# Four key products in other PSUM banks, in a two-layer graph kernel

## What is computed

```python
def layer0(h, adj):                       # Wq, Wk, Wv with biases
    query, key, value = h @ Wq.T + bq, h @ Wk.T + bk, h @ Wv.T + bv
    weight = adj * exp(query @ key.T)
    weight = weight / sum(weight, axis=2, keepdims=True)
    return weight @ value

def layer1(h, adj):
    agg = adj @ h / maximum(sum(adj, -1), 1e-6)
    return relu(concatenate([h, agg], axis=2) @ W.T)

x = x + layer0(maximum(layernorm(x), 0), adj)
x = x + layer1(maximum(layernorm(x), 0), adj)
```

## Time and profile before

| | us |
|---|---|
| median of 3 runs (2077.85 to 2078.81) | 2078.81 |
| span of the profiled execution | 2075.8 |
| TensorE busy in it | 2033.4 (98%) |
| DVE busy | 1420.9 (68%) |
| GpSimd busy | 1015.8 (49%) |
| ScalarE busy | 772.6 (37%) |

### The profile page before, as it was taken

How to read it: one execution, slowest core, us unless ns; L and a number is a source line. 1 busy time by engine, 2 the same in 40 slices (tenths; PEclk the granted TensorE clock), 3 DMA queues, 4 the chain that set the end, 5 groups by cost and what they waited for, 6 DMA issues and landing times.

```text
span 2075.8 us, 28517 instructions
## 1 busy us (share of the span) xinstructions
PE 2033.4 (98%) x9852; PEld 1702.4 (82%) x9852; DVE 1420.9 (68%) x2329; ACT 772.6 (37%) x1289; POOL 1015.8 (49%) x958
## 2 busy tenths in 40 slices
PE   8899999999999999999999999999999999999999
PEld 5688888888888888888888888888888888888887
DVE  6877676776667776767767677766677676767654
ACT  3433434333343334343333433344433334333432
POOL 3555553554544555535555445455355554454520
PEclk9999999999999999999999999999999999999999
DMA  5121122212222221222122221212221222212101
GB/s 188 61 76 67 66 76 91 81 51 76 72 85 81 70 72 66 76 91 81 51 72 75 86 81 65 76 66 76 91 81 51 71 76 86 81 60 82 63 29 51
DMA packets 114753, 155.30 MB, mean 75 GB/s; under 512 B 10800, under 2 KB 75312, under 8 KB 114736
## 3 DMA queue, kind: packets, MB, share of 16 engines
q1 hardware_dynamic: 114736, 155.08, 22.0%
HBM read 121.38 MB, written 33.68 MB: 75 GB/s over the span
## 4 chain that ended last, share of the span: by engine, by line
PE 87%; DVE 10%; issue 1%; DMA 0%; SPq 0%; ACT 0%; DVEq 0%; ACTq 0%
PE bank L337 28%; PE bank L339 28%; PE bank L338 28%; DVE hT_l L689 4%; PE bank L345 3%; DVE y L800 1%; DVE x L815 1%; DVE sums L834 1%; DVE h L831 1%; DVE h L730 0%; DMA x_in<-x 0%; DVE sum_inv L836 0%; DVE w_l L175 0%; DVE w L745 0%; DVE v_l L684 0%
## 5 line engine op out<-in xcount | busy, mean ns | idle before, releaser
L292 POOL TENSOR_TENSOR xT<-xT,shared 128x512 f32<-128x512 f32 x248 | 455.5, 1874 | 162.0 <-DMA shared<-norms 162.0
L325 POOL TENSOR_TENSOR at_l<-adjT,at_h 128x1024 fp32r<-128x1024 f32 x32 | 81.4, 2545 | 308.4 <-ACT at_h L675 308.4
L337 PE MATMUL bank<-hT_h,n_h 128*128 128x512 f32 x512 | 204.0, 399 | 23.6 <-DVE x L815 23.1
L269 POOL TENSOR_TENSOR rs<-var_eps,minus_half 128x2 f32<-128x2 f32 x128 | 89.7, 701 | 272.4 <-DVE var_eps L706 272.4
L730 DVE CUSTOM_DVE_ANT_0 h<-h,u_b,bqk 128x512 f32<-128x512 f32 x128 | 215.0, 1731 | 0.0
L535 ACT ACTIVATE h<-x,rs 128x512 f32<-128x512 f32 x124 | 94.1, 807 | 313.5 <-POOL rs L275 313.5
L579 ACT ACTIVATE y<-bank 128x512 f32<-128x512 f32 x128 | 76.7, 599 | 355.6 <-PE bank L339 355.6
L175 POOL TENSOR_TENSOR w_l<-w,w_h 128x512 fp32r<-128x512 f32 x62 | 80.4, 1297 | 255.1 <-ACT w_h L597 255.1
L338 PE MATMUL bank<-hT_l,n_h 128*128 128x512 f32 x512 | 200.3, 391 | 0.0
L339 PE MATMUL bank<-hT_h,n_l 128*128 128x512 f32 x512 | 200.1, 391 | 0.0
L337 PE MATMUL bank<-wv_h,hT_h 128*128 128x512 f32 x512 | 199.2, 389 | 0.0
(11 more groups left out here) (125 smaller groups left out, 4865.9 us busy)
## 6 DMA issues: line engine op xcount, KB each, us to landing
x_in<-x SPq DMA_DIRECT2D x32, 1024.0 KB, 5.3
xT<-x_t SPq DMA_DIRECT2D x62, 512.0 KB, 6.6
out<-x SPq DMA_DIRECT2D x124, 256.0 KB, 2.0
adjT<-adj_t SPq DMA_DIRECT2D x32, 512.0 KB, 3.5
shared<-adj SPq DMA_DIRECT2D x32, 512.0 KB, 4.8
shared<-norms SPq DMA_DIRECT2D x31, 512.0 KB, 3.6
x<-wq SPq DMA_DIRECT2D x4, 256.0 KB, 3.8
xb<-wk SPq DMA_DIRECT2D x4, 256.0 KB, 4.4
```

The costliest lines, as they stand in the source:

```text
L269: pool.tensor_tensor(rs[n][:, 0, tiles], var_eps[n][:, tiles], minus_half[:, :], ALU.pow).then_inc(rstd_done[n], 1)
L292: pool.tensor_tensor(tile, tile, norms[:, k * T:(k + 1) * T, :], (ALU.mult, ALU.add)[k]).then_inc((xT_scaled, xT_shifted)[k], 1)
L325: pool.tensor_tensor(at_l[:, :, :], adjT[:, :, :], at_h[:, :, :].bitcast(F32), ALU.subtract).then_inc(at_split, 1)
L337: pe.matmul(dst, lh, rh, start=first, stop=False)
```

## The change

The four key products get a list of banks of their own, 7, 4, 5 and 2. Their readers, line 569 on ScalarE and line 776 on DVE, read there. The waits of TensorE follow the last reader of each bank: in the steps with layer 1, kp(0) waits only for hT_split, kp(1) for ha_copied, kp(2) for y_done, and kp(3) for the first x1_done. turn_g(1), which writes bank 7, waits for the first kz_l. scores(0) and scores(1) write banks 0 and 1, and the first of them now waits for all four x1_done. In step 0, kp(1) waits for the copies of the bias columns and kp(2) for u_done. The order of instructions is the same on every engine; on TensorE a few register instructions that serve the waits come and go.

```diff
@@ -35,6 +35,7 @@
 L0_BANK, L1_BANK, TR_BANK = 0, 4, 6
+KP_BANK = (7, 4, 5, 2)
@@ -382,11 +383,22 @@
                 def kp(dt):
-                    pe.wait_ge(hT_split, DT * (i + 1))
-                    if layer1:
-                        pe.wait_ge(x1_done, T * j + dt + 1)
+                    if dt == 0:
+                        pe.wait_ge(hT_split, DT * (i + 1))
+                    elif dt == 1:
+                        if not layer1:
+                            pe.wait_ge(bias_columns_done, 2)
+                        elif not first:
+                            pe.wait_ge(ha_copied, T * j)
+                    elif dt == 2:
+                        if not layer1:
+                            pe.wait_ge(u_done, 1)
+                        elif not first:
+                            pe.wait_ge(y_done, T * j)
+                    elif layer1:
+                        pe.wait_ge(x1_done, T * j + 1)
                     cols = slice(dt * P, (dt + 1) * P)
-                    product(bank[L0_BANK + (dt + 2) % 4][:, :],
+                    product(bank[KP_BANK[dt]][:, :],
                             [(n_h[:, c, cols], n_l[:, c, cols], hT_h[:, c, :], hT_l[:, c, :]) for c in range(DT)]
                             ).then_inc(kp_psum, 1)
@@ -407,6 +419,8 @@
                         if g == 0 and kt == 0:
+                            if layer1:
+                                pe.wait_ge(x1_done, T * (j + 1))
                             pe.wait_ge(kp_split, DT * i + DT - 1)
                             product(dst, terms[:-1], stop=False)
                             pe.wait_ge(kp_split, DT * (i + 1))
@@ -485,6 +499,7 @@
                     kp(3)
                     if layer1:
                         turn_g(j, 0)
+                        pe.wait_ge(kp_split, DT * i + 1)
                         turn_g(j, 1)
                     scores(0)
@@ -566,7 +581,7 @@
-                    nc.scalar.activation(kz_h[:, dt, :], bank[L0_BANK + (dt + 2) % 4][:, :], ACT.Identity,
+                    nc.scalar.activation(kz_h[:, dt, :], bank[KP_BANK[dt]][:, :], ACT.Identity,
                                          bias=kp_bias[:, dt:dt + 1]).then_inc(kp_high, 1)
@@ -773,7 +788,7 @@
-                    nc.vector.scalar_tensor_tensor(out=kz_l[:, dt, :], in0=bank[L0_BANK + (dt + 2) % 4][:, :],
+                    nc.vector.scalar_tensor_tensor(out=kz_l[:, dt, :], in0=bank[KP_BANK[dt]][:, :],
                                                    scalar=kp_bias[:, dt:dt + 1], in1=kz_h[:, dt, :].bitcast(F32),
                                                    op0=ALU.add, op1=ALU.subtract).then_inc(kp_split, 1)
```

## The result

| | before, us | after, us |
|---|---|---|
| median of the runs (4 each) | 2078.60 | 2046.13 |
| range of the runs | 2077.85 to 2078.81 | 2045.16 to 2046.55 |
| span of the profiled execution | 2075.8 | 2044.8 |
| TensorE busy | 2033.4 (98%) | 2023.7 (99%) |

The ratio of the times is 0.9845, with a 95% interval from 0.9831 to 0.9859. That is 32.5 us less, where 32.6 were forecast. The spans differ by 31.0 us only, because the setup of the profiled execution after was 1.4 us longer (DVE waited 14.5 us instead of 13.1 for its first x_in).

What follows compares the result with a forecast made beforehand. TensorE was taken to bound the kernel, with one recurring pause before kp(0). Gains of 32.7 and 0.35 us (33.0 in all) less 0.4 in step 0 give 32.6 less: 2078.81 to 2046.2 us, range 2044.0 to 2053.0.

Steps and rivals of the forecast that it cites:

- The pause and the restart: Before kp(0) in each step: 0.91 us of pause and 0.18 of slower matmuls, 1.09 us gained, 30 times, 32.7 us.
- the first 0.11 only: In kp(0): if the slow pace after the first matmul, 0.07 us a step, were not restart, 2.1 us would stay.
- Loop entry, step 0 and step 1: Before the loop's steady turns: step 0 loses 0.4 us; at i = 1, at half clock, 0.35 us is gained.
- The new wait in step 0: kp(1) waits for the bias columns in bank 4, starts at 31.94, and costs 0.37 us with restart; bounds 0 and 3.
- Loop exit: At the loop's exit: the same gain of 1.09 us as in each of the 29 turns, 0.18 of it restart.
- Cover: At kp(0): hT_l ends 1.24 us before the last attention matmul starts; the other three products' waits are covered by over 1 us.
- The tightest place: At the first score product, which needs kz_l of kp(2): 0.31 us left after the signal.
- A: At the scores: TensorE waits for kz_l of kp(2), losing 0.3 to 0.7 us a step; 2057 to 2067 us; 9 in 100.
- B: At kp(0): held by hT_split until about 1027.4, or TensorE needs the pause; 2077 to 2080 us; 3 in 100.
- C: At weigh(0) on DVE: collides with GpSimd's additions to xb, net +0.6 us a step; about 2097 us; 2 in 100.
- D: More gain by the clock or its earlier rise at i = 1: 2 to 6 us more, 2040 to 2044; 4 in 100.

Runs made afterwards that it cites:

- the last four runs above: Changed kernel plus a 256-column DVE instruction, 2045.20 us; 512 columns, 2053.07; GpSimd's at_l after the first x1, 2045.91; that with 512 columns, 2045.58.
- the one with the new wait, the 512-column run: Changed kernel plus an idle 512-column DVE instruction ahead of kz_l of kp(2): 2053.07 us.
- The dose of DVE work: Changed kernel plus one idle DVE instruction ahead of kz_l of kp(2): 2045.20 us with 256 columns, 2053.07 us with 512.
- the three kernels that end at the same time by different means: The change, 2046.13 us; kernel before with kp(0) alone in bank 7, 2045.94; kernel before with GpSimd's at_l after the first x1, 2045.33.
- pauses of 2.13 us: Changed kernel with its new banks, but kp(0) waits for the second x1_done: 2123.6 us.
- the edit on the reader's side: Changed kernel with GpSimd's at_l started only after the first x1: 2045.91 us.

## Why the prediction was right

The place and the mechanism were right: one wait for a shared bank, closed in every step. The terms follow one by one, on the distance from the first key product of the program to the last step (1952.7 us before, 1920.4 after):

- **The pause and the restart, 1.09 us a step.** The step went from 63.503 to 62.420 us, 1.083 us less; 29 times that is 31.4 us. kp(0) at 2.72 us confirms that the whole 0.18 belonged to the restart and not the first 0.11 only.
- **Loop entry, step 0 and step 1.** From the first key product to the one of step 2 it is 111.13 us before and 110.24 after: 0.89 us less, which includes the pause at the start of step 2 (0.92). Forecast: 0.35 - 0.4 + 0.91 = 0.86. The new wait in step 0 shows as forecast, as a weight load held by the bias columns (weight loads of TensorE):

```profile
33.29 0.19 PEld L338 LDWEIGHTS bank<-hT_h,n_h 128*128 128x128 f32 x1 [0.44 <-DVE bqk L781]
```

  kp(1) starts 0.40 us after the last matmul of kp(0) instead of 0.23, and takes 2.87 us instead of 2.72: 0.32 us, where 0.37 were worked out. The clock did not fall at it. At i = 1 the first two matmuls of kp(0) run at half clock, the clock rises at about 76.9 (48.2 us after the first key product, against 47.8 before), and the gain is 0.49 - 0.21 = 0.3 us; forecast 0.35.
- **Loop exit.** The restart of the last kp(0), 0.10 us; forecast 0.18.

That is 31.4 + 0.9 + 0.1 = 32.4 us, and the medians give 32.5. That the sum is met to 0.1 us is in part luck. The runs of one kernel scatter by over 1 us, and the way to step 2 takes from 109.7 to 110.2 us in the five profiled executions with these banks and waits (the change and the last four runs above), and the clock rises at another moment in each, from 73.9 to 77.2 us. The 0.89 us of the entry could as well have been 1.4. The loop term isn't open to that: it is the same in all of them but the one with the new wait.

**Cover**, the time by which an input is ready before it is asked for. hT_split and the other new waits held nobody in the loop. The tightest place was named rightly: kz_l of kp(2) ends at 1024.11, and the scores' weight load stands here (TensorE's weight loads):

```profile
1023.48 1.02 PEld L346 LDWEIGHTS bank<-ident,h 128*128 128x128 f32 x8
1024.48 0.19 PEld L338 LDWEIGHTS bank<-hT_h,kz_h 128*128 128x128 f32 x1
```

The distance is 0.37 us, of which 0.06 go to the signal: 0.31 us, as forecast. The dose of DVE work gives 0.33.

**Rivals.**

- A (the scores catch TensorE) was a real mechanism, as the 512-column run shows, but began 0.3 us further on.
- B (the wait only changes its name) is refuted by the absence of any wait in the loop and by the three kernels that end at the same time by different means.
- C (GpSimd's additions meet weigh(0)) did not occur: the multiplications of weigh take 0.69 us in the whole span. The lock itself is real, since moving at_l took hT_l from 2.88 to 0.68 us, which agrees with the exclusive pair of ports in the Trainium skill ("SBUF — State Buffer", section "SBUF: two separate sides").
- D (more than forecast, by the clock) did not occur: with its pauses of 0.76 us the loop before already ran at a granted clock of 1.00, and at i = 1 the clock rose no earlier. With pauses of 2.13 us the clock did fall, in two of 29 turns, and rise again. A clock that falls and rises because of small pauses between groups of matmuls is what the Trainium skill describes ("TensorE: Matmul & The Clock Gate", section "A second HAM failure mode: psum-queue depth-cycling"); the traces here agree with it at 2.13 us of pause and show nothing of it at 0.76.

The one thing that the prediction didn't see is how little of the change its gain needs: it treats the four products alike, though its own rows show that only kp(0) was held.

## What to carry to other kernels

A buffer that two stages share costs time only where the second stage asks for it before the first stage's reader is done. Look for the single wait that is not covered and move that one buffer. Price the pause from start to start of the matmuls, with the slow ones behind it, and read every turn of the loop: a typical one can miss a clock that falls in a few. Before moving a buffer ask why its reader is late: here one GpSimd instruction, whose result TensorE uses only in the next step, held DVE for 2.2 us, and holding it back won the same time. After the gain, measure how far the next wait is, by a dose of idle work ahead of it. Here it was 0.3 us, and the edit on the reader's side widened it to over 1 us.

## What was not expected of the hardware

- At a granted clock of 1.00 a restart of TensorE costs 0.13 to 0.18 us (12 matmuls in 2.85 to 2.90 us instead of 2.72) behind pauses of 0.76 and of 2.14 us alike, and nearly nothing behind one of 0.2 us.
- A DVE instruction put into the queue moves what follows by less than its duration: 0.32 us for one of 0.40, 0.58 us for one of 0.66.
- Pauses of 0.76 us left the granted clock at 1.00 in every turn. Pauses of 2.13 us did so in 27 turns of 29; in two the clock fell to 0.50 for some 3 us, and each cost about 1.6 us more. In step 1, with 2.1 us more of pause, the clock fell back soon after it had risen, and kp(0) took 1.2 us longer.
